# x and the context in two layouts in memory: keys and normed x split from the one with dimension on partitions

## What is computed

```python
Q = einsum('btx,dx->btd', layernorm(x), Wq) + bq
K = einsum('bpx,dx->bpd', ctx, Wk) + bk
attn = softmax(einsum('btd,bpd->btp', Q, K) / 32)
x = x + einsum('btp,bpd->btd', attn, ctx)
h = silu(layernorm(x) @ Wg.T) * (layernorm(x) @ Wu.T)      # 3584 wide, weights decoded from 4-bit codes
x = x + h @ Wd.T
```

## Time and profile before

| what | before |
|---|---|
| median of 3 runs | 1981.54 us (1979.77 to 1982.28) |
| the profiled execution: first to last instruction | 1973.9 us |
| granted TensorE clock, mean | 0.997 |
| PE busy | 1928.0 us, 98% |
| DVE busy | 1637.0 us, 83% |
| ACT busy | 1484.2 us, 75% |
| POOL busy | 404.3 us, 20% |

### The profile page before, as it was taken

One profiled execution on the slowest core, in us unless ns is written; L12 is line 12 of the kernel. 1 busy time (PEld: TensorE's weight loads), 2 busy tenths in 40 slices (PEclk: granted clock), 3 DMA queues, 4 the chain that ended last, 5 costly groups with the idle time before them and its releaser, 6 DMA issues.

```text
span 1973.9 us, 29877 instructions
## 1 busy us (share of the span) xinstructions
PE 1928.0 (98%) x9872; PEld 983.3 (50%) x9872; DVE 1637.0 (83%) x2758; ACT 1484.2 (75%) x2758; POOL 404.3 (20%) x600
## 2 busy tenths in 40 slices
PE   8989999989999999999999999999999999999999
PEld 3468878754444444444444444444444444444444
DVE  6757888986988988988988998898898898996963
ACT  3767886757889889889889889889899999900000
POOL 0022464441211211211211211111123222201110
PEclk9999999999999999999999999999999999999999
DMA  9112689683555555554544644645569899893562
GB/s 346 30 49 65 170 233 233 180 299 72 140 127 119 148 125 124 148 130 113 156 122 117 156 127 113 150 129 120 137 176 239 230 216 247 217 274 117 173 224 85
DMA packets 393626, 314.63 MB, mean 159 GB/s; under 512 B 327296, under 2 KB 327296, under 8 KB 391552
## 3 DMA queue, kind: packets, MB, share of 16 engines
q1 hardware_dynamic: 347360, 159.07, 35.2%
q0 software_dynamic: 44032, 153.65, 23.9%
q10 hardware_dynamic: 2080, 0.01, 0.1%
HBM read 154.31 MB, written 82.31 MB: 120 GB/s over the span
## 4 chain that ended last, share of the span: by engine, by line
PE 53%; ACT 22%; DVE 12%; issue 6%; DMA 1%; DVEq 0%; ACTq 0%; POOL 0%
PE ps L2125 38%; PE ps L2167 12%; ACT sq L346 7%; ACT sq L342 5%; ACT w L346 2%; DVE w L362 2%; ACT w L342 2%; PE ps L1494 1%; ACT halves L414 1%; PE ps L1569 1%; DVE tail L2277 1%; ACT tail L2198 1%; ACT T L1664 1%; PE ps L1533 1%; DVE tail L1219 1%
## 5 line engine op out<-in xcount | busy, mean ns | idle before, releaser
L2125 PE MATMUL ps<-T,wS 128*128 128x512 f16 x4704 | 1017.6, 379 | 4.1 <-DVE ps L2232 2.5
L2125 PEld LDWEIGHTS ps<-T,wS 128*128 128x128 f16 x4704 | 459.8, 98 | 558.4 <-issue 4.9
L346 ACT ACTIVATE sq<-sq 128x512 f32<-128x512 f32 x898 | 516.2, 627 | 0.0
L362 DVE SCALAR_TENSOR_TENSOR w<-sq,w 128x512 f32<-128x512 f32 x590 | 417.3, 707 | 109.5 <-ACT sq L346 99.6
L342 ACT ACTIVATE sq<-q 128x512 f32<-128x512 int32 x598 | 362.9, 631 | 49.6 <-DVE w L362 47.5
L2167 PE MATMUL ps<-T,tail 128*128 128x512 f16 x1584 | 345.0, 379 | 5.3 <-issue 2.1
L2167 PEld LDWEIGHTS ps<-T,tail 128*128 128x128 f16 x1584 | 154.6, 98 | 193.3 <-issue 5.9
L1533 PE MATMUL ps<-T 128*128 128x256 f16 x1536 | 174.1, 273 | 4.2 <-DVE T L1760 4.1
L2167 PE MATMUL ps<-T,wS 128*128 128x512 f16 x768 | 168.5, 379 | 1.0 <-DMA T<-halves 1.0
L430 DVE SCALAR_TENSOR_TENSOR halves<-w,halves 128x512 f16<-128x512 f32 x240 | 162.4, 686 | 6.4 <-ACT halves L414 6.2
L2073 POOL DMA_DIRECT2D keep_h<-tail x196 | 106.3, 542 | 295.7 <-DVE tail L2277 293.6
(11 more groups left out here) (226 smaller groups left out, 1936.8 us busy)
## 6 DMA issues: line engine op xcount, KB each, us to landing
keep_h<-tail POOLq DMA_DIRECT2D x196, 256.0 KB, 2.5
tail<-keep_h POOLq DMA_DIRECT2D x66, 512.0 KB, 5.0
wS<-keep_h POOLq DMA_DIRECT2D x32, 512.0 KB, 4.8
q<-in_L_ffn_down_q POOLq DMA_DIRECT2D x56, 256.0 KB, 4.2
q<-in_L_ffn_up_q POOLq DMA_DIRECT2D x52, 256.0 KB, 2.9
q<-in_L_ffn_gate_q POOLq DMA_DIRECT2D x48, 256.0 KB, 3.4
keep_x<-T SPq DMA_DIRECT2D x38, 256.0 KB, 3.2
T<-in_x SPq DMA_DIRECT2D x9, 1024.0 KB, 5.6
```

The source lines that it names most:

```text
L346: nc.scalar.activation(place, place, ACT.Square, bias=b, scale=a).then_inc(un.s_act, 1)
L362: nc.vector.scalar_tensor_tensor(out=out, in0=square_place(un, u, i - 1), scalar=FACTORS[i - 1][1], in1=un.w[:, buf, :], op0=ALU.add, op1= ...
L2125: last = nc.tensor.matmul(ps[:, bank, :], un.wS[:, z % SLOTS, a, kt, :], t.Tp[side][product][:, :, b, kt, :], start=fresh and n == 0, stop ...
```

## The change

`kernel()` now lays out x and the context twice in memory before the launch: as rows (`x_rows`, `ctx_4096_rows`) and with the dimension first (`x_cols`, `ctx_4096_cols`: partition, eighth of the dimension, row). The turned layouts are loaded by DMA into `xT` and `key_cols`. So:

- The transposes of the keys (all 8 steps) and of x (steps 0 to 6, for the next batch) leave PE. Only the x of batch 0 is still normed as rows and transposed, in front of step 0.
- The layer norm of x in the turned layout needs rstd and shift of each row along the free axis: PE transposes them, spread over 128 columns (`turn_norm`, 4 transposes for each batch from 1 on), ACT copies the bank to `norm` (`norm_rows`), and POOL multiplies and adds (`x_scale`, `x_shift`, 2 of each for a batch, 128 x 1024 each, in place in `xT`), after o = 0 to 3 of the step before. ACT and DVE then split `xT` (`x_hi`, at o = 3 and 6, and `x_lo`).
- `keys_hi` and `keys_lo` split `key_cols` directly (2 instructions of 128 x 1024 each instead of 4 of 128 x 512 from PSUM). The rows of the context are still needed by `attended`: they are loaded once more, and split one step later (`key_rows_hi` at o = 1 and 2, `key_rows_lo` at o = 4 and 5).
- `bias_dots` reads the unnormed rows of x, and the norm is put into the small terms (`row_terms`); it now stands behind `residual`, right ahead of `key_max`. The probabilities are transposed after o = 5 instead of o = 1.
- The order of some late loads and waits at the end of step 7 follows.

The core of the diff:

```diff
-        t.xnT = big(32, 8).rearrange("p (a k t) -> p a k t", a=2, k=KT)
+        t.xnT = [place.rearrange("p (a k t) -> p a k t", a=2, k=KT) for place in (big(32, 8), small(0, 8).bitcast(F16))]
...
-        t.keys16 = big(88, 16).rearrange("p (b a i d) -> p b a i d", b=2, a=2, i=TB)
+        t.keys16 = [place.rearrange("p (a i d) -> p a i d", a=2, i=TB) for place in (big(88, 8), big(32, 8))]
         t.keys16_rows = big(88, 16).bitcast(F32).rearrange("p (k d) -> p k d", k=4)
-        t.keys = big(104, 8).bitcast(F32).rearrange("p (i d) -> p i d", i=TB)
+        t.keys = big(96, 8).bitcast(F32).rearrange("p (i d) -> p i d", i=TB)
+        t.key_cols = big(104, 8).bitcast(F32).rearrange("p (k t) -> p k t", k=KT)
+        t.first_rows = big(104, 8).bitcast(F32).rearrange("p (i d) -> p i d", i=TB)
+        t.xT = big(72, 8).bitcast(F32).rearrange("p (k t) -> p k t", k=KT)
...
-            if b >= 2 and b + 2 < BATCH:
-
-                sp.wait_ge(s_xn, TB * b if b == 2 else TB * (b + 1))
-                sp.dma_start(x_feed(b + 2), t.x_t[:, TB * (b + 2):TB * (b + 3), :]).then_inc(s_xf, 16)
...
+            if more:
+                sp.wait_ge(s_ktlo, HALVES * (b + 1))
+                sp.dma_start(key_cols[:, :, :], t.ctx_cols[b + 1]).then_inc(s_keys, 16)
...
-            if b < LAST:
-
-                sp.wait_ge(s_t, 2 * XG * (b + 1))
-                sp.wait_ge(s_klo, TB * (b + 1))
-                sp.dma_start(keys[:, :, :], t.ctx_t[b + 1]).then_inc(s_keys, 16)
+            if b + 2 < BATCH:
+                sp.wait_ge(s_xlo, x_split(b + 1))
+                sp.dma_start(xT[:, :, :], t.x_cols[b + 2]).then_inc(s_xcols, 16)
...
+            if b > 0:
+                load_key_rows(b)
...
+        def x_scale(b, h):
+
+            pool.wait_ge(s_xcols, 16 * b)
+            pool.wait_ge(s_norm, b)
+            nc.gpsimd.tensor_tensor(x_half(h), x_half(h), norm[:, 0:SEQ].rearrange("p (o t) -> p o t", o=1).broadcast_to([P, 4, SEQ]),
+                                    ALU.mult).then_inc(s_scaled, 1)
+
+        def x_shift(b, h):
+
+            pool.wait_ge(s_scaled, HALVES * (b - 1) + h + 1)
+            nc.gpsimd.tensor_tensor(x_half(h), x_half(h), norm[:, SEQ:2 * SEQ].rearrange("p (o t) -> p o t", o=1).broadcast_to([P, 4, SEQ]),
+                                    ALU.add).then_inc(s_shifted, 1)
+
+        def key_rows_lo(b, i):
+
+            pool.wait_ge(s_khi, TB * b + i + 1)
+            nc.gpsimd.tensor_tensor(keys16(b)[:, 1, i, :], keys[:, i, :], keys16(b)[:, 0, i, :], ALU.subtract).then_inc(s_klo, 1)
...
-                if o in KEYS_LO_AT:
-                    i = KEYS_LO_AT.index(o)
-                    pool.wait_ge(s_khi, TB * b + i + 1)
-                    nc.gpsimd.tensor_tensor(keys16[:, b % 2, 1, i, :], keys[:, i, :], keys16[:, b % 2, 0, i, :],
-                                            ALU.subtract).then_inc(s_klo, 1)
+                if o < 4 and b < LAST:
+                    (x_shift if o % 2 else x_scale)(b + 1, o // 2)
+                if o in KEYS_LO_AT and b > 0:
+                    key_rows_lo(b - 1, KEYS_LO_AT.index(o))
...
+        def turn_norm(b):
+
+            wait(pe, s_norm, b - 2)
+            for j, stat in enumerate((t.rstd, t.shift)):
+                for i in range(TB):
+                    n = TB * b + i
+                    last = nc.tensor.transpose(ps[:, norm_bank(b), (j * TB + i) * P:(j * TB + i + 1) * P],
+                                               stat[:, n:n + 1].broadcast_to([P, P]), ident[:, :])
+            last.then_inc(s_norm_t, 1)
...
                 if o == PROBS_AT and b > 0:
                     turn_probs(b - 1)
-                if o in KEYS_AT:
-                    turn_keys(b, o - KEYS_AT[0])
-            if more:
-                turn_x(b + 1, 0)
...
-        def x_hi(b, g):
-            act.wait_ge(s_t, 2 * XG * b + g + 1)
-            nc.scalar.copy(x_group(b, g)[1][0], ps[:, x_bank(b, g), :].rearrange("p (k t) -> p k t", k=4)).then_inc(s_xhi, 1)
-
-        def x_normalise(b, i):
-
-            if b >= 4:
-                act.wait_ge(s_xf, 16 * (b - 3))
-            act.wait_ge(s_t, 2 * XG * (b - 1) + HALVES * (i + 1))
-            act.wait_ge(s_dot, TB * b)
-            n = TB * b + i
-            nc.scalar.activation(xn[:, i, :], x_feed(b)[:, i, :], ACT.Identity, scale=t.rstd[:, n:n + 1],
-                                 bias=t.shift[:, n:n + 1]).then_inc(s_xn, 1)
-
-        def keys_hi(b, i):
+        def first_x_hi(g):
+            act.wait_ge(s_t, g + 1)
+            nc.scalar.copy(x_group(g)[1][0], ps[:, x_bank(g), :].rearrange("p (k t) -> p k t", k=4)).then_inc(s_xhi, 1)
+
+        def x_hi(b, h):
+
+            act.wait_ge(s_shifted, HALVES * (b - 1) + h + 1)
+            if b == 1:
+                act.wait_ge(s_t, XG)
+            wait(act, s_r, KT * (b - 1))
+            nc.scalar.copy(xnT(b)[:, 0, 4 * h:4 * h + 4, :], x_half(h)).then_inc(s_xhi, 1)
+
+        def norm_rows(b):
+
+            act.wait_ge(s_norm_t, b)
+            wait(act, s_shifted, HALVES * (b - 1))
+            wait(act, s_dot, TB * (b - 1))
+            nc.scalar.copy(norm[:, :], ps[:, norm_bank(b), :]).then_inc(s_norm, 1)
+
+        def key_rows_hi(b, i):
+
+            act.wait_ge(s_krows, 16 * (b + 1))
+            wait(act, s_att, ATT * b if b < LAST else 0)
+            scale = k_in[:, b % 2:b % 2 + 1]
+            nc.scalar.activation(keys16(b)[:, 0, i, :], keys[:, i, :], ACT.Copy, scale=scale)
+            nc.scalar.activation(keys[:, i, :], keys[:, i, :], ACT.Copy, scale=scale).then_inc(s_khi, 1)
+
+        def keys_hi(b, h):
 
             act.wait_ge(s_kin, b + 1)
-            nc.scalar.activation(keys16[:, b % 2, 0, i, :], keys[:, i, :], ACT.Copy, scale=k_in[:, 0:1])
-            nc.scalar.activation(keys[:, i, :], keys[:, i, :], ACT.Copy, scale=k_in[:, 0:1]).then_inc(s_khi, 1)
-
-        def turned_keys_hi(b, g):
-            i, h = g // HALVES, g % HALVES
-            act.wait_ge(s_t, 2 * XG * b + XG + g + 1)
-            nc.scalar.copy(keysT[:, 0, 4 * h:4 * h + 4, i * P:(i + 1) * P],
-                           ps[:, g % 2, :].rearrange("p (k t) -> p k t", k=4)).then_inc(s_kev, 1)
+            wait(act, s_scores, TB * b)
+            nc.scalar.activation(keysT[:, 0, 4 * h:4 * h + 4, :], key_cols[:, 4 * h:4 * h + 4, :], ACT.Copy,
+                                 scale=k_in[:, b % 2:b % 2 + 1]).then_inc(s_kthi, 1)
...
+                if b == 0 and o == 0:
+                    norm_rows(1)
+                if o in KEYS_HI_AT and b > 0:
+                    key_rows_hi(b - 1, KEYS_HI_AT.index(o))
+                if o in X_HI_AT and more:
+                    x_hi(b + 1, X_HI_AT.index(o))
+                if o in KEYS_T_AT:
+                    keys_hi(b, KEYS_T_AT.index(o))
...
+            if b + 2 < BATCH:
+                norm_rows(b + 2)
...
+        def x_lo(b, h):
+
+            dve.wait_ge(s_xhi, x_split(b - 1) + h + 1)
+            nc.vector.tensor_tensor(xnT(b)[:, 1, 4 * h:4 * h + 4, :], x_half(h), xnT(b)[:, 0, 4 * h:4 * h + 4, :],
                                     ALU.subtract).then_inc(s_xlo, 1)
...
+            wait(dve, s_khi, TB * (b - 1))
...
+            streams.dve.run(base + 3)
+            if more:
+                x_lo(b + 1, 0)
+            streams.dve.run(base + 4)
+            keys_lo(b, 0)
+            streams.dve.run(base + 5)
+            keys_lo(b, 1)
+            streams.dve.run(base + 6)
+            if old:
+                t_lo(nc, dve, t, c, 0)
+            if more:
+                x_lo(b + 1, 1)
             if b > 0:
                 probs_lo(b - 1)
-                if more:
-                    bias_dots(b + 1)
             else:
-                dve.wait_ge(s_bias, 1)
-                bias_dots(0)
-            streams.dve.run(base + 3)
-            for g in range(XG):
-                keys_lo(b, g)
-                if old and g >= 2:
-                    t_lo(nc, dve, t, c, g - 2)
-                streams.dve.run(base + 4 + g)
-            if more:
-                x_lo(b + 1, 0)
-            else:
+                row_terms()
+            if old:
+                t_lo(nc, dve, t, c, 1)
+            streams.dve.run(base + 7)
...
+            bias_dots(b)
             if more:
-                x_lo(b + 1, 2)
                 key_max(b + 1)
...
+    laid = {name: np.asarray(inputs[name]) for name in _INS}
+    for name in ("x", "ctx_4096"):
+        a = laid.pop(name)
+        laid[name + "_rows"] = a.reshape(NT, P, DIM).transpose(1, 0, 2)
+        laid[name + "_cols"] = a.reshape(BATCH, SEQ, KT, P).transpose(0, 3, 2, 1)
+    for name in ("x_rows", "x_cols", "ctx_4096_rows", "ctx_4096_cols", *_INS[2:]):
+        a = np.ascontiguousarray(laid[name])
...
```

219 lines of the change are left out of this document (105 added, 114 removed).

## The result

The changed kernel takes 2064.09 us (median of 4 runs, 2059.32 to 2068.12) against 1981.91 us (4 runs, 1979.77 to 1986.44): ratio 1.0425, 95% interval 1.0395 to 1.0456. The prediction had the direction, the place and most of the mechanism; the size, +37 us, was less than half of the +82 measured, and the time lies outside the range of 1988 to 2044 us.

A forecast was written before the change was run, and what follows sets the result against it. POOL's list with its reduction and the chain through ACT, DVE and PE were to bound `attend`. Step 0 0, step 1 +2, steps 2 to 6 +38, step 7 -4, end +1 gave +37: span 2010.9, median 2018.5 us, range 1988 to 2044.

The forecast's parts named there:

- P: Start of POOL's first low part in a step of `attend`; one such start to the next was 37.1 us before.
- I take 3 us for both together, and a period of 45.5: Steps 2 to 6: lower bound 42.4 us plus 3 for engine interference and PE's clock; bounds 42.4 and 49.
- `attended` from P + 18.0: PE in each step: four groups of 5.2 us in all, each behind its eviction, from P + 18.0 to P + 23.2.
- to P + 17.9: DVE in each step: `x_lo` and `probs_lo` done 17.9 us after P.
- The interference term of 1 to 3 us: Each step: POOL and DVE hold each other up, adding 1 to 3 us to the period.
- 10.7 us from `attended` to `kmax` done: Each step: `attended` 5.2 us, then DVE's last residual 0.7, two `bias_dots` of 1.25 and `key_max` 2.27, to P + 28.7.
- The clock, half of the 3 us: PE at `attended`: half clock after a 10 us gap in each step, lying in the chain, costing 1 to 3 us.
- With the 7.6 us between span and median: Whole kernel: 7.6 us added to the forecast span of 2010.9 us to give the median, 2018.5 us.
- nearer to 47 than to 43: Period by the port lock rule: four DVE instructions in the chain wait 1.25 us in two of three cases, 3.3 us.
- Rival (a): PE stays the bound, faster than before: steps go down towards 32.3 us, -30 us, 1951 us; chance 8%.
- (b): PE's gain and POOL's loss cancel, periods of 37 to 38 us, 1977 to 1986 us; chance 5%.
- (c): The `key_cols` transfer becomes late for `key_max`: periods 2 to 4 us longer, 2030 to 2038 us; chance 12%.

The follow-up runs named there:

- no_x_work: Changed kernel without `x_scale` and `x_shift`, POOL's four 128x1024 instructions a step (another output): 2010.09 us, ratio 1.0151.
- klo_on_dve: Changed kernel with the low parts of the key rows formed by DVE ahead of `x_lo`, not by POOL: 2048.43 us, ratio 1.0345.
- pe_kept_busy_128: Changed kernel with 128 more matmuls on PE in each of steps 1 to 6, behind R and ahead of `attended`: 2059.92 us, ratio 1.0429.
- kmax_early: Changed kernel with DVE forming the next batch's largest key ahead of the residuals and `bias_dots`: 2047.49 us, ratio 1.0341.
- kmax_turned: Changed kernel with POOL's seven reductions replaced by a PE transpose and a DVE maximum over 128 columns: 2048.42 us, ratio 1.0338.
- kmax_early_held: Changed kernel with the largest key formed ahead of the residuals and POOL's `x_scale` held until y's norm scales are ready: 2047.42 us, ratio 1.0342.

## Why the prediction was right in kind and wrong in size

Right: the step is set by POOL's list and chains through it, not by PE; ACT's wait ahead of L1643 (6.27 us, put down to POOL L1454, at P + 5.9 where 6.3 was forecast); both gaps of the reduction unchanged; `x_scale` and `x_shift` at 2.34 to 3.32 us; a lower clock in the stretch. no_x_work shows that these instructions carry most of the loss. Two of the signs named did not come: POOL was to have almost no other idle time, and it waits 6.56 us for `kmax`; PE was to be idle some 10 us ahead of L1541, and it was 14.70.

Where the 80 us of `attend` lie, up to the end of `attended(7)`, against the +37 of the sum: up to P of step 1, +1.3 (forecast 0); step 1, 51.6 us, +11.5 (+2); steps 2 to 6, +60.5 (+38); step 7 to its last score, -0.6 (-4); the end, +7.6 (+1).

The step that failed is the period of steps 2 to 6, "42.4 as the lower bound" and "I take 3 us for both together, and a period of 45.5". Measured in step 4, P to P is 50.3:

- **`attended` from P + 18.0.** It started at P + 22.1. The evictions came as forecast, the last at P + 16.9. But the chain named them, `x_lo` and `probs_lo` alone as what `attended(b - 1, 0)` waits for; it also waits for `key_rows_lo` on POOL (`s_klo`), which the change puts behind the four x instructions, and that ended at P + 22.0. This wait was missed. klo_on_dve shows that naming it would not have been enough: DVE's queue up to `probs_lo` ends at P + 20.6, also too late.
- **"to P + 17.9" for `x_lo` and `probs_lo`.** The sum took DVE as free there. From 322.04 DVE had seven instructions before `probs_lo` was done, 13.3 us of durations where 7.0 are their shortest. The interference term of 1 to 3 us was meant for all of it; the held up instructions cost 6.3 us on DVE ahead of `attended` and, on POOL, 29.1 us for a list that the prediction had at 28. That was the mis-sized term.
- **10.7 us from `attended` to `kmax` done.** It was 13.5: DVE waited for a split of y behind POOL's `t_sum` before the first residual. The prediction counted the residuals from PE's side only.
- **The clock, half of the 3 us.** It does happen (6.97 us instead of 5.2), and pe_kept_busy_128 shows that it costs nothing in steps 2 to 6, as `attended` is not what the residuals wait for there.
- **13.7 us of reduction.** It was 14.7 in step 4, and 13.7 to 14.7 over the seven.
- **"With the 7.6 us between span and median".** In each run listed the time is 1.8 us above its span; the profiled execution before was itself some 6 us below the median. The two profiled spans differ by 88.1 us, 80.3 of them in `attend`. Nearly all of the other 8 lie between 1805 and 1840 us, where PE waits for transfers; the kernel before scatters from 1969 to 1991 us in its other runs, so this is not put down to the change.

So 4.1 + 2.8 + 1.0 us on top of 42.4 make the 50.3. Step 1 was taken as 42 us "without a second norm"; there DVE has pieces of the weight stream ahead of `probs_lo` that POOL holds up in the same way (two of 2.61 us, two of 1.95), PE waits 21.58 us, and the step is the longest of all. At the end the price of the exponents behind the context rows was taken as 1 us of a range up to 5; it was 6.0, and 1.6 more for the lower clock of `attended(7)`.

By the rule of the Trainium skill (SBUF — State Buffer, section Who interferes with whom) the prediction gave a period "nearer to 47 than to 43". That estimate was the better one, though still 3 us short. The rule had been applied to four instructions in the chain only; in step 4 the other instructions with two SBUF inputs that DVE queues ahead of `attended` were held up as well (`keys_lo` at 1.69 and 2.77 us for 1.28, the stream piece at 1.15 for 0.68).

Rival (a), PE as the bound, did not occur: in no order tried did PE become the bound. Rivals (b) and (c) did not occur in the changed kernel.

## What to carry to other kernels

A wait in front of the next product has several semaphores; after a move, follow each of them through the queue of its engine, also those that were long done before. Work taken from PE and PSUM and given to elementwise engines that read SBUF cost twice here: its own time, and that of the DVE instructions which POOL's then held up, down to those on two columns. And when removing a wait brings a third of what it was worth, look for a second queue that ends within a microsecond of the first: here POOL's list, DVE's and the reduction lay so close that none of the three moves klo_on_dve, kmax_early and kmax_turned gave more than 17 us. Only taking the x instructions off POOL gave more by itself, 40 us with DVE doing them.

## What the runs showed of the hardware

- A chain of 17 DVE instructions on 128x2, each using what an earlier one wrote, took 3.5 us with POOL waiting (kmax_early_held) and 15.1 us beside POOL instructions of 2.35 us (kmax_early).
- One reduction over the partitions takes POOL out for 13.7 to 14.7 us, each of the 7 times in the changed kernel, and its row shows 0.38 us. One PE transpose (0.27 us) with a maximum over 128 columns (0.28 us) gives the same value. It saved nothing in the kernel before, where POOL waits 4.9 to 8.7 us a step for `kmax` anyway.
- PE's granted clock fell to 0.50 behind a wait of 4.75 us, although 11 us of matmuls stood ahead of it, and the same 24 matmuls took 8.03 us. With 14 us of matmuls ahead they took 7.03 us behind waits of 3.0 to 3.9 us, and 5.34 us behind waits of 0.58 and 1.45 us.
